# Depthwise convolution in four column tiles of 32 pixels, its output turned in 32x32 blocks on VectorE, and ScalarE emptying whole expand pairs

## The reference

```python
h = jnp.einsum('oc,bchw->bohw', w1, x)                 # expand, 48 -> 288 channels
h = jax.nn.relu(_bn(h, g1, b1, m1, v1))
h = jax.lax.conv_general_dilated(h, wd, window_strides=(1, 1), padding=((1, 1), (1, 1)),
        feature_group_count=HID, dimension_numbers=('NCHW', 'OIHW', 'NCHW'))   # depthwise 3 x 3
h = jax.nn.relu(_bn(h, gd, bd, md, vd))
h = jnp.einsum('oc,bchw->bohw', w2, h)                 # project, 288 -> 48 channels
h = _bn(h, g2, b2, m2, v2)
return x + h
```

## Time and profile before

| | us |
|---|---|
| median of 3 runs | 1955.76 (1953.94 to 1955.84) |
| span of the profiled execution | 1952.0 |
| PE busy | 1870.2 (96%) |
| DVE busy | 1445.8 (74%) |
| ACT busy | 1322.8 (68%) |
| POOL busy | 647.1 (33%) |

### The profile page before, as it was taken

One profiled execution on the slowest core, in us unless ns is written; L12 is line 12 of the kernel. 1 busy time (PEld: TensorE's weight loads), 2 busy tenths in 40 slices (PEclk: granted clock), 3 DMA queues, 4 the chain that ended last, 5 costly groups with the idle time before them and its releaser, 6 DMA issues.

```text
span 1952.0 us, 74705 instructions
## 1 busy us (share of the span) xinstructions
PE 1870.2 (96%) x29960; PEld 1565.2 (80%) x29960; DVE 1445.8 (74%) x2650; ACT 1322.8 (68%) x2838; POOL 647.1 (33%) x869
## 2 busy tenths in 40 slices
PE   5999999999999996999999999999999999999998
PEld 4888888888888885555555899999999999999997
DVE  5999999999999997666667556566566566566564
ACT  2788878878888885555555666666666666666665
POOL 4333333333333333413100434325334343344240
PEclk9999999999999998999999999999999999999999
DMA  2222222222222222777664444545363454445331
GB/s 67 68 73 76 78 73 76 77 73 76 77 72 77 74 76 77 182 171 179 161 150 111 97 108 126 99 113 126 87 147 86 112 137 102 103 129 105 99 111 34
DMA packets 286410, 198.43 MB, mean 102 GB/s; under 512 B 225991, under 2 KB 275672, under 8 KB 276504
## 3 DMA queue, kind: packets, MB, share of 16 engines
q1 hardware_dynamic: 282114, 189.12, 37.9%
q0 software_dynamic: 2368, 6.25, 1.5%
q10 hardware_dynamic: 1750, 0.39, 0.1%
HBM read 128.36 MB, written 54.72 MB: 94 GB/s over the span
## 4 chain that ended last, share of the span: by engine, by line
PE 56%; ACT 2%; DMA 1%; issue 1%; DVE 0%; SPq 0%; ACTq 0%; DVEq 0%
PE psum L1126 14%; PE psum L1145 13%; PE psum L1171 9%; PE psum L1180 5%; PE psum L680 5%; PE psum L661 3%; PE psum L651 3%; PE psum L666 2%; ACT h2T L1227 1%; DMA room<-tok_mid 1%; ACT h L884 1%; DMA room<-in_ident 0%; ACT room L750 0%; DVE room L885 0%; DVE room L712 0%
## 5 line engine op out<-in xcount | busy, mean ns | idle before, releaser
L934 POOL TENSOR_TENSOR mats<-mats,dscale 112x2048 f32<-112x2048 f32 x72 | 260.8, 3622 | 315.0 <-DMA mats<-in_taps 312.6
L1126 PE MATMUL psum<-ew,xp 64*100 64x96 f32 x6144 | 322.4, 252 | 16.8 <-ACT h L884 13.5
L885 DVE TENSOR_SCALAR h<-psum 100x384 f32<-100x384 f32 x384 | 211.9, 557 | 151.7 <-PE psum L1126 141.6
L1126 PEld LDWEIGHTS psum<-ew,xp 64*100 64x100 f32 x6144 | 295.5, 165 | 26.3 <-ACT h L884 18.6
L1227 ACT ACTIVATE h2T<-psum 96x1024 f32<-96x1024 f32 x192 | 195.6, 1019 | 177.5 <-PE psum L1180 177.5
L1145 PE MATMUL psum<-h,mats 101*64 101x128 f32 x4608 | 269.2, 274 | 1.6 <-issue 0.9
L1145 PEld LDWEIGHTS psum<-h,mats 101*64 101x64 f32 x4608 | 252.0, 137 | 11.8 <-issue 2.0
L884 ACT ACTIVATE room<-psum 64x512 f32<-64x512 f32 (+1 forms) x384 | 206.1, 537 | 78.1 <-PE psum L1145 71.5
L344 PE MATMUL psum<-kb,qa 128*64 128x256 f32 x2048 | 244.0, 380 | 0.8 <-DVE prob L443 0.8
L885 DVE TENSOR_SCALAR room<-psum 64x512 f32<-64x512 f32 (+1 forms) x288 | 174.2, 605 | 64.7 <-PE psum L1145 58.8
L884 ACT ACTIVATE h<-psum 100x384 f32<-100x384 f32 x384 | 186.6, 486 | 48.1 <-PE psum L1126 34.1
(11 more groups left out here) (154 smaller groups left out, 3228.3 us busy)
## 6 DMA issues: line engine op xcount, KB each, us to landing
mats<-in_taps SPq DMA_DIRECT2D x69, 896.0 KB, 5.9
tok_mid<-mid SPq DMA_DIRECT2D x128, 224.0 KB, 1.9
room<-tok_mid SPq DMA_DIRECT2D x64, 448.0 KB, 4.4
piece<-img_mid SPq DMA_DIRECT2D x196, 63.8 KB, 2.4
img_mid<-room SPq DMA_DIRECT2D x128, 97.5 KB, 3.0
kb<-kk SPq DMA_DIRECT2D x512, 24.0 KB
out<-yc SPq DMA_DIRECT2D x32, 384.0 KB, 4.5
scratch<-in_x_tokens SPq DMA_DIRECT2D x126, 96.0 KB, 1.9
```

The costliest lines, as they stand in the source:

```text
L885: return nc.vector.tensor_scalar(dst, src, 0.0, None, ALU.max)
L934: nc.gpsimd.tensor_tensor(m, m, bc(scale[0:MROWS, at:at + TCH], 2, POUT), ALU.mult).then_inc(mats_scaled, 1)
L1126: mm = nc.tensor.matmul(ring[(j + u) % 4][0:PIN, p:4 * CH:4], xp[hx][rows, 2 * j + p, :], w1[rows, c, :], start=True, stop=True)
```

## The change

- Depthwise uses four column tiles of 32 pixels in place of two of 64. A channel is two matmuls (pixels 0 to 31 and 32 to 63, index b), each of 32 weight columns and 128 moving columns, and four channels (index j) run on the four tiles. A unit still has 16 channels, and is now a pair of banks, one per b, with 128 partitions in use: 32 j + pixel.
- PSUM is now a ring of three pairs of banks, which expand pairs and depthwise units share. An expand pair holds r = 0 and r = 1, and is emptied as a whole, 100 x 768, by ACT. Depthwise units are emptied as a whole, 128 x 1024, by ACT (0, 2, 4) and DVE (1, 3, 5).
- The turn leaves PE and ACT. In each step DVE transposes 128 x 1024 values of `h2` in blocks of 32 x 32 into one of four `h2T` buffers, all in SBUF. A block of 32 rows holds 24 channels and 8 values beyond them, for which the projection's weights are zero (`placed_rows`).
- A projection step is 2 matmuls of 512 columns. On PE they follow 6, 4, 4 and 2 expand pairs, two steps at a time; the first depthwise unit of the next chunk comes after the last projection.

The core of the diff:

```diff
-EXPANDS = PATCHES // 4
+EXPANDS = PATCHES // 8
+PAIRS_OUT = EXPANDS + DEPTHS
+QUAD = 32
+LANES = CH // 4
...
-        ring = [psum[:, s, :] for s in range(4)]
-        ps_t = psum[:, 4:6, :]
+        ring = [psum[:, 2 * t:2 * t + 2, :] for t in range(3)]
...
+        EXPANDED = (6, 4, 4, 2)
...
+        def by_act(u):
+            return u % PAIRS_OUT < EXPANDS or (u % PAIRS_OUT - EXPANDS) % 2 == 0
...
+        def evacuate_expand(k, i):
+            u = expand_at(k, i)
+            dst = h1[0:PIN, :, :].rearrange("q c (r p) -> q r c p", r=2)[:, :, :, 4 * i:4 * i + 4]
+            relu(by_act(u), dst, ring[u % 3][0:PIN, :, 0:4 * CH].rearrange("q r (c p) -> q r c p", p=4))
+        def evacuate_depthwise(k, d):
+            u = depth_at(k, d)
+            dst = h2[:, :, :, 4 * d:4 * d + 4].rearrange("q p b n -> q b p n")
+            relu(by_act(u), dst, ring[u % 3].rearrange("q b (p n) -> q b p n", n=4))
...
+            def pair_free(u):
+                if u >= 3:
+                    pe.wait_ge(*emptied_by(u - 3))
...
-                for n in range(DUNIT // 2):
-                    for u in range(2):
-                        ch = DUNIT * d + DUNIT // 2 * u + n
-                        bank = psum[POUT * u:POUT * u + POUT, 4 * (d % 2) + u + 2 * (n // 4), :]
-                        mm = nc.tensor.matmul(bank[:, n % 4:4 * PATCHES:4], mats[ch // TCH][0:PIN + 1, ch % TCH, :],
-                                              h1[0:PIN + 1, ch, :], start=True, stop=True)
+                for n in range(4):
+                    for b in range(2):
+                        for j in range(4):
+                            ch = DUNIT * d + 4 * j + n
+                            mm = nc.tensor.matmul(ring[u % 3][QUAD * j:QUAD * j + QUAD, b, n:4 * PATCHES:4],
+                                                  mats[ch // TCH][0:PIN + 1, ch % TCH, QUAD * b:QUAD * b + QUAD],
+                                                  h1[0:PIN + 1, ch, :], start=True, stop=True)
...
+                for n in range(NSTEP):
+                    if not last and n % 2 == 0:
+                        for i in units_at(n // 2):
+                            expand(k + 1, (c + 1) % CHUNKS, (hx + 1) % 2 if c == CHUNKS - 1 else hx, i)
                     pe.wait_ge(copied, NSTEP * k + n + 1)
+                    if NSTEP * k + n >= 2:
                         pe.wait_ge(y_done, NSTEP * k + n)
+                    for r in range(2):
+                        mm = nc.tensor.matmul(ps_y[n % 2][64 * r:64 * r + 64, :], w2[:, c, :], h2T[n % TURNS][:, r, :],
+                                              start=True, stop=True)
                     mm.then_inc(y_ready, 1)
+                if not last:
+                    depthwise(k + 1, 0)
...
+            def turn(n, k):
+                pc, a, m = STEPS[n]
+                if n == 0:
+                    for d in (DEPTHS - 2, DEPTHS - 1):
+                        dve.wait_ge(*emptied_by(depth_at(k, d)))
+                wait(dve, y_ready, NSTEP * k + n - TURNS + 1)
...
+                nc.vector.transpose(h2T[n % TURNS].rearrange("q r (p x) -> q r p x", x=QUAD), src).then_inc(copied, 1)
...
+                for d in range(1, DEPTHS, 2):
+                    filtered(k, d)
+                for n in range(NSTEP + 2):
+                    if n >= 2:
+                        add(n - 2, b, hx, c, k)
+                    if n < NSTEP:
+                        turn(n, k)
```

More of the change, by code:

```diff
@@ L892, in evacuate_depthwise, with expand_at @@
[L892 to L898, removed]
+        def expand_at(k, i):
+            return PAIRS_OUT * k + i
@@ new lines, in depth_at, with emptied_by, relu @@
+        def depth_at(k, d):
+            return PAIRS_OUT * k + EXPANDS + d
+        def by_act(u):
+            return u % PAIRS_OUT < EXPANDS or (u % PAIRS_OUT - EXPANDS) % 2 == 0
+        def emptied_by(u):
+            n = sum(by_act(v) == by_act(u) for v in range(PAIRS_OUT))
+            rest = sum(by_act(v) == by_act(u) for v in range(u % PAIRS_OUT + 1))
+            return unit_act if by_act(u) else unit_dve, n * (u // PAIRS_OUT) + rest
+        def relu(act, dst, src):
+            if act:
+                return nc.scalar.activation(dst, src, ACT.Relu).then_inc(unit_act, 1)
+            return nc.vector.tensor_scalar(dst, src, 0.0, None, ALU.max).then_inc(unit_dve, 1)
@@ L1154, in first @@
                 pe.wait_ge(border_set, 2)
-                for j in range(0, EXPANDS, 2):
-                    expand(0, 0, 0, j)
-                depthwise(0, 0)
+                for i in range(EXPANDS):
+                    expand(0, 0, 0, i)
             def chunk(b, hx, c, last):
                 k = number(b, hx, c)
-                for u in range(1, DEPTHS):
+                for u in range(0 if k == 0 else 1, DEPTHS):
                     depthwise(k, u)
@@ L1173, in project @@
                     mm.then_inc(y_ready, 1)
-                def turn(n):
-                    pc, a, _ = STEPS[n]
-                    for p in range(PART):
-                        for r in range(2):
-                            rows = slice(POUT * r, POUT * r + POUT)
-                            mm = nc.tensor.transpose(turned_at(n, last)[0:CH, r, POUT * p:POUT * p + POUT],
-                                                     h2[rows, PR * pc + a + p, :], ident[rows, rows])
-                    mm.then_inc(turned, 1)
@@ L1184, in chunk @@
-                if last:
-                    emptied(k, DEPTHS)
-                    turn(0)
-                    for n in range(NSTEP):
-                        if n + 1 < NSTEP:
-                            turn(n + 1)
-                        project(n)
-                    return
-                for n in range(NSTEP + 1):
-                    for j in units_at(n):
-                        ahead = NSTEP * k + n if n % 2 and n < NSTEP - 1 and j == units_at(n)[-1] else 0
-                        expand(k + 1, (c + 1) % CHUNKS, (hx + 1) % 2 if c == CHUNKS - 1 else hx, j, ahead)
-                    if n == NSTEP:
-                        depthwise(k + 1, 0)
-                    for m in projected_at(n):
-                        project(m)
-                    if n < NSTEP:
-                        turn(n)
+                if not last:
+                    depthwise(k + 1, 0)
@@ L1307, in placed_taps, with placed_rows @@
     return placed
+def placed_rows(w2T):
+    rows = np.zeros((CHUNKS, 4, QUAD, C), np.float32)
+    rows[:, :, 0:LANES, :] = w2T.reshape(CHUNKS, DEPTHS, 4, 4, C).transpose(0, 2, 1, 3, 4).reshape(CHUNKS, 4, LANES, C)
+    return rows.reshape(CHUNKS, P, C)
 def kernel(**inputs):
```

160 lines of the change are left out of this document (48 added, 112 removed).

## The result

The changed kernel takes 1880.13 us (median of 4 runs, 1879.91 to 1888.86) against 1954.94 for the kernel before on the same chip: a ratio of 0.9628, 95% interval 0.9608 to 0.9648. It is faster by 75 us. I had predicted 1834, a gain of 122; the result lies inside the range of 1818 to 1885, but 46 us above the number.

What follows compares the result with a forecast made beforehand. PE, busy for 96% of the span, bounds the kernel. Expand 11.3, depthwise 10.8, projection 7.0, tiling 0.7 and wait 0.8 make 30.6 us a chunk against 35.98; 23 chunks save 122, giving 1834 us, range 1818 to 1885.

Steps and rivals of the forecast that it cites:

- Turns leave PE, with their waits: PE, each chunk: 3.82 us of turning go, and with them the two waits, 1.0 us.
- Depthwise at four tiles, 10.8: Depthwise on PE: four column tiles run at once, 96 steps of 0.113, 10.8 us a chunk, as before.
- the four 64x64 tiles of the earlier trace: MLP's matmuls: eight records of 256 columns over after 0.66 us, taken as showing four moving streams at once.
- Expand 11.3, projection 7.0, changes of tiling 0.7: PE, per chunk: 16 expand pairs 11.3 us, eight projections of 0.87 make 7.0, tiling changes not in these 0.7.
- The wait before projection 7, 0.8: End of a chunk: PE ready at 18.4, the last turn on DVE done at 19.2, so PE waits about 0.8 us.
- Evacuations and the turn hidden or priced right: ACT and DVE: expand pair 806 ns, depthwise units 1.02 and 1.23 us, evacuations hidden behind PE; turn on DVE 1.22.
- Rival B: Turn on DVE is dear: at 2.3 us a chunk takes 36.1, time 1965; decides from 2.2 on; chance 0.08.
- The ends unchanged: First expand of all 14.2 us against 14.3 now; last chunk, a chain on DVE, 17.8 against 17.6.
- It holds for the 23 chunks: Loop over chunks: the saving of 5.3 us applies to all 23 chunks with a successor, 122 us.
- Rival A: Depthwise: four tiles not kept fed or run two by two; decides above 0.165 us per four, up to 2085; chance 0.12.
- Rival C: Next half's pieces or taps come late: overdrawn by 2 to 4 us in 7 halves, 1850 to 1860; chance 0.06.

Runs made afterwards that it cites:

- small taps: The changed kernel, but each taps load in the loop over chunks moves only 16 rows of one channel (4 KB for 896 KB): 1826.16 us, ratio 0.9359.
- the ordered transfers: The changed kernel, all work done, but after depthwise the output's second half is stored, then taps loaded, with pieces two deep: 1834.88 us, ratio 0.9388.

## Why the prediction was right, and where 46 us went

- **Turns leave PE, with their waits**: right. No turn and neither of the two waits is left on PE in the chunks.
- **Depthwise at four tiles, 10.8**: right, 10.62. The argument from the four 64x64 tiles of the earlier trace rows held for four column tiles.
- **Expand 11.3, projection 7.0, changes of tiling 0.7**: 19.0 together, and 19.7 in the kernel with small taps (19.91 from the end of depthwise to the next, less the wait of 0.22). Off by 0.7.
- **The wait before projection 7, 0.8**: 0.22 to 0.34. The mistakes cancel: 30.6 predicted, 30.52 in an undisturbed chunk. (35.98 less 30.6 is 5.4 and not 5.3, so the sum should have said 124 and not 122.)
- **Evacuations and the turn hidden or priced right**: right, see the groups above. Rival B falls. Its own price was added up wrong: 24.6 + 1.4 + 1.0 and 10.8 of depthwise are 37.8 and not 36.1 a chunk, which counts only the six adds that stand before the last turn.
- **The ends unchanged**: right within 2 us or so. The first depthwise starts at 1087.01 (1087.52 before); the last chunk takes 33.3 from the start of its depthwise to the end (35.5 before).
- **"It holds for the 23 chunks"**: this is the step that failed. It held for five of the 23. The sum had no term for the fetch of instructions, which put it at nothing without a reason: it cost 33.5 us of stops and up to 15 of half clock, and 54 us in all by the run with small taps. With that term at zero the kernel takes 1826 to 1827 in two ways, and 1829 to 1830 by their ratios to the 1955.76 of the prediction, so the rest of the sum was right within 4 to 8 us. That the ordered transfers give 1834.88 is luck: that run still has waits for the border and a drop of the clock. It is luck too that the result fell inside the range, which reached up to 1885 for other causes, the border and the mild halves of rivals A and B.
- **Rival A ("not kept fed")** named the new density, 28 ns a record where the densest stretch that it had found ran at 42, but looked for its price in PE: a step longer than 0.165. The step is 0.111. The density was paid for in another place, where SP's loads meet PE's instructions. The Trainium skill ("Runtime: NRT & Kernel Launch", Instruction fetch mechanics) says that blocks of 256 instructions are fetched ahead and that this is mostly hidden. The trace agrees on the block, and disagrees on the hiding once the DMA engines are full and a block lasts 3.5 us.
- **Rival C (pieces or taps late)**: hardly in the changed kernel, where POOL's border made PE's weight loads wait 0.4 us in all. But it is what spoils each simple remedy: moving the taps back by some microseconds used up the slack that I had worked out at 3.6 and 8 us.

What stays open: 5 to 7 of the 56 us are unaccounted for (gaps under 0.15 us add up to only 0.2), and which stop brings the clock down can't be told from its length alone.

## What to carry to other kernels

When a change makes an engine's instructions denser, work out how long a block of 256 lasts there and read the DMA share of that stretch: with large loads outstanding, fetches went out up to 5.9 us late here, and a block that lasted 6 us or more could bear a delay of up to 4.5. Keep large loads out of the densest stretch, and check what stands behind them on their queue when they are moved. Price a stop of PE of about 2 us at its length plus a stretch of half clock, 3.4 us as a rule, which came with 13 of 23 waits in one run here and with 7 of 10 stops of 1.75 us or more in another.

## What the hardware showed that I had not expected

- A fetch of 16 KB that takes 1.2 us started some 5.6 us late, with three loads of 896 KB issued just before, at 247 GB/s and a DMA share of 0.96; PE resumed 1.4 us after its end.
- Stops of 1.6 to 3.3 us from a plain semaphore wait brought the granted clock to 0.50 for 3.41 or 6.83 us, with 13 of the 23 waits in that run.
- At half the instruction rate fetches were still up to 4.5 us late, and PE never stopped at the end of a block.
- Two column tiles of 32 take 0.087 us a pair, two of 64 take 0.111 (10.65 us for 96 pairs), and four of 32 take 0.111.
- STREAM_TRANSPOSE of 128x1024 four-byte elements in 32x32 blocks costs 1229 ns, the same as a plain pass by DVE.
